# Layer 2 mixture: up weights resident in SBUF, a tile's columns copied by VectorE

## The reference, cut to what matters

```
B, S, D, F, E, K = (8, 1024, 128, 512, 8, 2)
shared = gelu(x @ W1s + b1s) @ W2s + b2s
rw = softmax(x @ Wr);  topw, topi = top_k(rw, K)
h    = gelu(einsum('bsd,edf->bsef', x, W1p) + b1p)
priv = einsum('bsef,efd->bsed', h, W2p) + b2p
out  = shared + sum over the two chosen experts of topw * priv
```

## Time and profile before

| what | value |
|---|---|
| time, median of 3 runs | 2392.99 us (2389.83 to 2393.37) |
| time of the profiled execution | 2382.97 us |
| its span, first to last instruction | 2381.2 us |
| TensorE clock granted over the span | 0.830 of full |
| PE / DVE / ACT / POOL busy | 75% / 51% / 37% / 32% |
| expert block of layer 2: first transpose, last bias addition | 1516.7 us, 1830.4 us |
| DMA traffic in it | 54.10 MB, mean 171 GB/s |

### The profile page before, as it was taken

One profiled execution on the slowest core, in us unless ns is written; L12 is line 12 of the kernel. 1 busy time (PEld: TensorE's weight loads), 2 busy tenths in 40 slices (PEclk: granted clock), 3 DMA queues, 4 the chain that ended last, 5 costly groups with the idle time before them and its releaser, 6 DMA issues. The chain is left out here.

```text
span 2381.2 us, 46310 instructions
## 1 busy us (share of the span) xinstructions
PE 1778.7 (75%) x12847; PEld 1424.4 (60%) x12847; DVE 1222.8 (51%) x4445; ACT 870.8 (37%) x2627; POOL 763.7 (32%) x1119
## 2 busy tenths in 40 slices
PE   5658999967499667777776994599996777347873
PEld 4546777756489556666664773488886566224331
DVE  5663333389656566888886542222221788512110
ACT  2333444424366424444443431255543233112220
POOL 3430000034256451000001677244443255413332
PEclk8889999988799858999998997799999577555555
DMA  2100000011133200000002111366665421112222
GB/s 73 53 19 6 1 1 1 1 34 31 32 117 117 56 0 1 0 0 0 0 0 64 37 48 53 103 177 175 176 174 146 111 68 34 42 51 64 62 62 98
DMA packets 156917, 136.22 MB, mean 57 GB/s; under 512 B 27474, under 2 KB 130659, under 8 KB 156675
## 3 DMA queue, kind: packets, MB, share of 16 engines
q1 hardware_dynamic: 143170, 106.15, 15.9%
q0 software_dynamic: 13568, 27.98, 3.5%
HBM read 100.70 MB, written 37.54 MB: 58 GB/s over the span
## 5 line engine op out<-in xcount | busy, mean ns | idle before, releaser
L1429 ACT ACTIVATE FEAT<-BANKS,EXP 128x128 f32<-128x128 f32 x544 | 155.0, 368 | 230.4 <-PE BANKS L1406 229.5
L1047 ACT ACTIVATE EXP<-BANKS,NEGMAX 128x128 f32<-128x128 f32 x512 | 138.9, 382 | 191.3 <-DVE NEGMAX L1059 191.3
L1360 POOL DMA_INDIRECT scratch_made<-FEAT x136 | 130.2, 958 | 198.0 <-DVE FEAT L1489 194.8
L195 PE MATMUL BANKS<-ident,WA 128*128 128x128 f32 x256 | 61.5, 385 | 161.9 <-DVE WA L189 161.8
L1406 PE MATMUL BANKS<-FEAT 128*128 128x128 f32 x1088 | 153.0, 284 | 16.3 <-issue 8.0
L1489 DVE TENSOR_TENSOR FEAT<-BANKS,B2BC 128x128 f32<-128x128 f32 x136 | 39.6, 291 | 241.4 <-PE BANKS L1415 241.4
L1406 PEld LDWEIGHTS BANKS<-FEAT 128*128 128x128 f32 x1088 | 133.4, 193 | 34.8 <-issue 26.3
L1826 POOL DMA_INDIRECT scratch_made<-FEAT x96 | 91.9, 957 | 191.7 <-DVE FEAT L1985 169.5
L1415 PE MATMUL BANKS<-AUX,FEAT 128*128 x1088 | 152.5, 283 | 0.5 <-ACT FEAT L1429 0.4
L412 PE MATMUL BANKS<-FEAT,ident 128*128 128x256 f32 x588 | 149.9, 383 | 0.0
L195 PEld LDWEIGHTS BANKS<-ident,WA 128*128 128x128 f32 x256 | 42.0, 196 | 173.3 <-DVE WA L189 135.9
(11 more groups left out here) (353 smaller groups left out, 4572.5 us busy)
## 6 DMA issues: line engine op xcount, KB each, us to landing
FEAT<-in_L_ffn_W1p SPq DMA_DIRECT2D x136, 256.0 KB, 2.7
EXP<-in_L_ffn_W SPq DMA_DIRECT2D x128, 128.0 KB, 2.0
FEAT<-scratch_sent SPq DMA_DIRECT2D x136, 64.5 KB
STAGE<-in_adj SPq DMA_DIRECT2D x32, 256.0 KB, 2.8
EXP<-scratch_made SPq DMA_DIRECT2D x32, 256.0 KB, 3.6
FEAT<-scratch_sent SPq DMA_DIRECT2D x96, 65.5 KB, 1.8
scratch_sent<-NONE SPq DMA_DIRECT2D x64, 65.5 KB, 1.6
X<-in_x SPq DMA_DIRECT2D x16, 256.0 KB, 3.1
```

Source lines behind the costliest of these rows:

```text
L195: last = pe.transpose(tile(ps, k), tile(src, k), ident[:])
L1047: last = act.activation(tile(EXS[:, par], 4 * k + n), tile(PS[j], c), ACT.Exp, bias=NEGMAX[:, par, 4 * k + n:4 * k + n + 1])
L1360: pool.indirect_dma_start(out=made2, out_offset=bass.IndirectOffsetOnAxis(ap=XI_I[:, t % R_IN, H:ROW2], axis=0), in_=YO[:, t % R_OUT, :], ...
L1429: last = act.activation(tile(HR[:, t % R_H], c), tile(PS[2 + t % 2], c), ACT.Gelu, bias=BT[:, c, t:t + 1])
```

## The change

All of `L2_ffn_W1p` (2 MB) is loaded once in the routing block into the lower half of `AUX` (`W1_2`, a fifth transfer on `load_e2`, ahead of `W2_2`). `first(t)` leaves SP and becomes a VectorE part: a `value_load` and a copy of 128 x 512 float32 from `W1_2` into the same ring `W1R` of 4. VectorE's `xT` becomes a ScalarE part ahead of `gelu`, with the same lag. VectorE's `result` goes from lag 2 to lag 3. The `value_load`s of this block lose `min_val` and `max_val`. The four semaphores of the weight ring become one.

```
+        W1_2 = AUX[:, 0:E2 * F2].rearrange("p (e f) -> p e f", e=E2)
...
+                sp.dma_start(W1_2, a["L2_ffn_W1p"].rearrange("e d f -> d e f")).then_inc(load_e2, 16)
                 sp.dma_start(W2_2, a["L2_ffn_W2p"].rearrange("e (c p) d -> p (e c) d", p=P)).then_inc(load_e2, 16)
...
                 def load(t):
-                    r = sp.value_load(ROWI[0:1, t:t + 1], min_val=0, max_val=ROWS2 - P)
+                    r = sp.value_load(ROWI[0:1, t:t + 1])
...
-                def first(t):
-                    e = sp.value_load(EOFI[0:1, t:t + 1], min_val=0, max_val=E2 - 1)
-                    reused(sp, s.h_ps, t, R_W)
-                    sp.dma_start(W1R[:, t % R_W, :], a["L2_ffn_W1p"][bass.ds(e, 1)].rearrange("o d f -> (o d) f")
-                                 ).then_inc(s_w1[t % R_W], 16)
                 sp.wait_ge(s.zr, 1)
                 for e in range(E2):
-                    r = sp.value_load(ZROW[0:1, e:e + 1], min_val=0, max_val=ROWS2 - P)
+                    r = sp.value_load(ZROW[0:1, e:e + 1])
...
-                in_turn(NT2, [(0, load), (1, first)])
+                in_turn(NT2, [(0, load)])
...
                 def up(t):
                     pe.wait_ge(s.xT, t + 1)
-                    pe.wait_ge(s_w1[t % R_W], 16 * (t // R_W + 1))
+                    pe.wait_ge(s.w1, t + 1)
...
                 def down(t):
-                    e = pe.value_load(EOFI[0:1, t:t + 1], min_val=0, max_val=E2 - 1)
+                    e = pe.value_load(EOFI[0:1, t:t + 1])
...
-                pe.wait_ge(load_e2, 4 * 16)
+                pe.wait_ge(load_e2, 5 * 16)
...
+                def xT(t):
+                    act.wait_ge(s.t_ps, t + 1)
+                    reused(act, s.h_ps, t, 3)
+                    act.copy(XTI[:, t % 3, :], PS[t % 2][:, 0:P]).then_inc(s.xT, 1)
                 act.wait_ge(s.bt, 1)
-                in_turn(NT2, [(1, gelu)])
+                in_turn(NT2, [(0, xT), (1, gelu)])
...
-                def xT(t):
-                    v.wait_ge(s.t_ps, t + 1)
-                    reused(v, s.h_ps, t, 3)
-                    v.tensor_copy(XTI[:, t % 3, :], PS[t % 2][:, 0:P]).then_inc(s.xT, 1)
+                def first(t):
+                    e = v.value_load(EOFI[0:1, t:t + 1])
+                    reused(v, s.h_ps, t, R_W)
+                    v.tensor_copy(W1R[:, t % R_W, :], W1_2[:, bass.ds(e, 1), :].rearrange("p a f -> p (a f)")).then_inc(s.w1, 1)
 
                 def result(t):
-                    e = v.value_load(EOFI[0:1, t:t + 1], min_val=0, max_val=E2 - 1)
+                    e = v.value_load(EOFI[0:1, t:t + 1])
...
-                in_turn(NT2, [(0, xT), (2, result)])
+                in_turn(NT2, [(0, first), (3, result)])
```

More of the change, by code:

```diff
@@ L1318, in program @@
         s = sems("ex2", "tot sh zr blank b0 ai bi nt tri cu ge sel prp prv dd row ex oneh bb bt b2 tab in0 in1 in2 in3 in4 in5 t_ps xT h_ps "
-                        "gelu y_ps y out0 out1 out2 out3 out4 out5 out6 out7 w1a w1b w1c w1d in6 in7")
+                        "gelu y_ps y out0 out1 out2 out3 out4 out5 out6 out7 w1 in6 in7")
         R_IN, R_OUT, R_H, R_W = 8, 8, 3, 4
@@ L1322, in program @@
         s_out = (s.out0, s.out1, s.out2, s.out3, s.out4, s.out5, s.out6, s.out7)
-        s_w1 = (s.w1a, s.w1b, s.w1c, s.w1d)
         room = lambda at, n: EXP[:, at:at + n]
@@ L1471, in _ @@
                 v.tensor_copy(ROWI[:], ROWF).then_inc(s.tab, 1)
-                v.wait_ge(load_e2, 4 * 16)
+                v.wait_ge(load_e2, 5 * 16)
                 v.tensor_tensor(B2BC[:], B2BC[:], B2SH[:].unsqueeze(1).to_broadcast([P, E2, H]), ALU.add).then_inc(s.b2, 1)
```

## The result

The change makes the kernel slower: 2430.45 us (2428.88 to 2433.17, 4 runs) against 2393.18 us (4 runs), a ratio of 1.0149 [1.0121, 1.0176], or +37.3 us. Predicted were 2340.5 us, range 2328 to 2363. The profiled execution took 2433.17 us, 50.2 us more than the profiled one before (2382.97).

The account below looks back on a forecast made before the run. The prediction took SP's issuing of two DMA series a tile as the expert block's bound. Savings of 48 (steady part), 4 (start) and 0.5 (end) made 52.5 us, so 2392.99 would become 2340.5 us, range 2328 to 2363.

Parts of the forecast that it names:

- What the change removes: Expert block: SP keeps one load series, 1.10 us a tile or about 0.83 without asserts; TensorE bounds next at 1.90.
- no assert on the load lines: Expert block: one of the signs that would show the forecast, the asserts gone with min_val and max_val.
- SP's issuing was the bound before: Expert block before the change: two series of SP issues make 2.20 us a tile; TensorE second, 0.37 us to spare.
- term of the steady part: Expert block: 132 steps shrinking from 2.269 to 1.90 us save 48.7 us, taken as 48.
- rival 3: Expert block: no gain, TensorE's 1.90 doesn't last or some engine gives the old pace; 2388 to 2398 us, chance 0.03.
- rival 2: Expert block: new cycle above 1.90, for example VectorE's copy held until the indirect DMA ends; 2353 to 2373 us, chance 0.18.
- Rival 4: Expert block: slower, VectorE's copy holds GpSimd's descriptors at the shared port; 2454 us, chance 0.05.
- The copy's price: VectorE in the expert block: the copy of 512 columns taken at 0.40 us, upper bound 0.69; no term.
- ScalarE's copy: ScalarE in the expert block: PSUM copy of 128 columns between 0.25 and 0.37 us, engine work 1.5 of 1.90; no term.
- The start of the block: Expert block's start: first transpose 2.4 us earlier, first up products 4.1 us earlier, or 1.8 if asserts stay; taken as 4.
- The early load: Routing block: one more 2 MB DMA on SP delays the blank writes at most another 5 us, hidden; zero.
- Rival 5: Expert block: more gain than forecast, because its DMA traffic falls by 34 MB; 2326 to 2334 us, chance 0.04.

Follow-up runs that it names:

- e4: Kernel before the change, with SP's three value_loads of the expert block losing min_val and max_val: ratio 0.9784 to the kernel before, pace 1.977 us a tile.
- e1: Changed kernel with min_val and max_val given back to every value_load of the expert block: ratio 0.9735 to the kernel before, pace 1.907 us a tile.
- e2: Changed kernel with bounds given back only to TensorE's one value_load (down products): ratio 0.9748 to the kernel before, pace 1.909 us a tile.
- e5: Changed kernel, the fourth of a tile's four down products reading weights at a fixed place: ratio 0.9863 to the kernel before, pace 2.134 us a tile.

## Why the prediction was wrong, point by point

**The step that failed** is in "What the change removes": "They stand on the `value_load` lines and the address has its own step, so I take them as gone; in the steady part it doesn't matter, since either is far under 1.90." I bounded the assert between gone and as before, and did so for SP, where it is right: the series there fell from 1.10 to (6.02 - 0.34) / 7 = 0.81 us, predicted 0.83. The blank writes and the first eight loads, kernel after:

```profile
1511.93 6.02 SPq L1378 DMA_DIRECT2D scratch_sent<-NONE  x8
...
1519.94 6.02 SPq L1373 DMA_DIRECT2D FEAT<-scratch_sent  x8
```

The same edit stood in PE's `down`, and I never asked what TensorE's sequencer does in a tile. I counted the sequencer of SP (the bound) and of VectorE (two loads), and took TensorE as 1.90 us of products. So the sentence "The next bound is TensorE with 1.90 us" fails with it: the next bound was TensorE's sequencer, with 2.60. The sign "no assert on the load lines" came true and meant less than I took it for: on SP the asserts were gone, on TensorE and VectorE they stood at the uses. The third case, that the bound moves to every use and so multiplies, was outside "gone or stays". Its price, had I thought of it: 4 x about 0.43 instead of one 0.17 and 4 x 0.125. That is 1.72 us instead of 0.67, 1.05 more on a sequencer whose slack nobody had counted; 0.70 of it came out above the 1.90. In the trace's cycle of 2.60 us the four uses take 1.71 from the first operation to the last, the register load 0.37 and three semaphore instructions 0.05 each; in the remaining 0.37 us the sequencer has no record.

**What held.**
- *SP's issuing was the bound before*: e4 frees SP alone and gains 2.2%.
- *TensorE's limit of 1.90*: 1.907 in e1, 1.909 in e2. The term of the steady part was 48 us; e1 measures 132 x (2.269 - 1.907) = 47.8. PE's 95% was no sign of a bound, and rival 3 doesn't occur.
- *No port problem at this pace and order.* The indirect DMA takes 0.960 us after, 0.957 before (medians). The timeline after has a copy that begins inside one:

```profile
1703.38 0.96 POOL L1361 DMA_INDIRECT scratch_made<-FEAT  x1 [1.62 <-DVE FEAT L1490]
...
1703.57 0.43 DVE L1483 COPY FEAT<-AUX 128x512 f32 x1 [0.47 <-PE BANKS L1402]
```

  The copy took its median 0.43 and ended before the DMA did, so it isn't held to the DMA's end, as rival 2 supposed; over all tiles 5 of the 136 copies took 0.63 to 0.64 us and the DMA was never longer than 0.991. Rival 4 had the right sign for a wrong reason, which is luck. The factor of five that the Trainium skill gives ("SBUF — State Buffer", "SBUF: two separate sides") isn't seen in any run here, but the runs hardly try it: in the kernel after 131 of the 136 copies begin inside a running indirect DMA and none begins ahead of one and reaches into it; the experiments have that order at most once each. What a copy that comes first does to the DMA is not shown.
- *The copy's price*: 0.40 taken, 0.427 measured. From the narrow casts I had 0.38, too low. The Trainium skill, "VectorE: DVE Perf Modes", section on the TRN2 errata, would have been nearer: its fixed term of about 150 cycles with two columns a cycle gives an estimate of (256 + 150) / 0.96 = 423 ns, and the trace agrees; its table row with 58 cycles gives an estimate of 327, which the trace contradicts.
- *ScalarE's copy*: 0.25 to 0.37 as bound, 0.267 measured:

```profile
L1432 ACT COPY FEAT<-BANKS 128x128 f32<-128x128 f32 x136 | 36.3, 267 | 146.7 <-PE BANKS L1395 146.7
```

- *The start of the block.* From the first counting product (1502.89 before, 1510.48 after) the first transpose comes 13.80 and then 11.44 us later, -2.4 as predicted, and the first up product 16.8 and then 12.4, -4.4 for a predicted 4.1. Kernel after:

```profile
1510.48 0.57 PE L1385 MATMUL BANKS<-CAR,ones 128*128 128x8 f32 x2 [48.85 <-PEq L101]
...
1521.92 0.45 PE L1395 MATMUL BANKS<-ident,FEAT 128*128 128x128 f32 x1 [1.72 <-DMA FEAT<-scratch_sent]
...
1522.84 2.02 PE L1402 MATMUL BANKS<-FEAT 128*128 128x128 f32 x8
```

- *The early load* holds SP in the routing block for 10.71 us instead of the 4.88 of the earlier trace rows, 5.8 more where I allowed 5, and it is hidden: from SP's first issue of the routing block to the first counting product are 222.9 us before and 223.1 after.

```profile
1290.96 10.71 SPq L1134 DMA_DIRECT2D B1P<-in_L_ffn_b1p  x1
```

With TensorE's bounds kept the forecast would have been about right: 1 - 52.5 / 2392.99 = 0.978 against 0.9748 [0.9707, 0.9788] of e2, which is that kernel, and 0.9735 [0.9701, 0.9769] of e1. The block gives 50.3 us of e1's gain (327.5 to 277.2), where its medians differ by 63.2; the remaining 13 us aren't located, since the kernel before has no trace in that set. Rival 5 had a gain beyond the forecast in mind; no run tests it. One sum of the prediction is slightly off without consequence: the first up products would come 4.1 - 2.4 = 1.7 us earlier if the asserts stayed, not 1.8.

## What to carry to other kernels

Count every engine's sequencer in a tile, not just its busy time: TensorE was 99% busy by its modelled ends while 133 matmul instructions ran where 182 can. For a register that addresses SBUF, state the bounds once at the load, above all if it is used several times; for one that only places a DMA, leave them out on the queue that is the bound. And when an edit of one word stands on several engines, cost it on each.

## What the runs showed of the hardware

- A `value_load` with bounds costs one register operation of 0.151 to 0.190 us and one assert of 0.018 to 0.023 at the load. Without bounds this pair appears at each use in an SBUF address (0.173 and 0.018 on TensorE, plus the 0.046 of the address; up to 0.218 and 0.023 on VectorE's addition), and at no DMA of this kernel. One use was worth 0.43 us by the records and 0.469 by e5, 0.06 of which is a shorter register load.
- The records of PE and its weight loads show of this only idle time in front of the down products' weight loads (61.6 us, 18.9 of it "by issue"), and so less busy time of these; the pace and the sequencer's own instructions name the cause.
- In e4 the issue of a 256 KB DMA held SP's queue for up to 1.03 us, and over 0.6 in 6 of 136 cases, where 0.33 is usual. Its cause stays open.
- A VectorE copy of 128x512 float32 that began inside a running indirect DMA took its median 0.427 us in the kernel after, at most 0.640.
